# A decoder layer in one program: the end of the self-attention in a new order (layer norm and gated layer first, last output products behind the second gated tile, four weight pieces behind batch 1's rows)

## The reference

```
x = x + attention(layernorm(x))          16 heads of 64, causal, output product with w_o
x = x + cross_attention(layernorm(x))    keys and values from 64 context rows per batch
x = x + ffn(layernorm(x))

ffn: h = silu(x w1 * s1) * (x w2 * s2)   "gated layer", 256 -> 1024, 8 tiles of 128
     h = gelu(h h1 * s)                  1024 -> 1024
     h = gelu(h h2 * s)                  1024 -> 1024
     out = h w3 * s3                     1024 -> 256
```

## Time and profile before

| | us |
|---|---|
| median of 3 runs | 1507.41 |
| lowest, highest | 1506.86, 1508.65 |
| the profiled execution, its own time | 1507.81 |
| its span | 1506.0 |
| TensorE busy in the span | 1487.9 (99%) |
| VectorE, ScalarE, GpSimd busy | 1101.3, 968.6, 492.1 |

### The profile page before, as it was taken

One profiled execution on the slowest core, in us unless ns is written; L12 is line 12 of the kernel. 1 busy time (PEld: TensorE's weight loads), 2 busy tenths in 40 slices (PEclk: granted clock), 3 DMA queues, 4 the chain that ended last, 5 costly groups with the idle time before them and its releaser, 6 DMA issues.

```text
span 1506.0 us, 29162 instructions
## 1 busy us (share of the span) xinstructions
PE 1487.9 (99%) x10680; PEld 1262.7 (84%) x10680; DVE 1101.3 (73%) x2772; ACT 968.6 (64%) x2274; POOL 492.1 (33%) x763
## 2 busy tenths in 40 slices
PE   8999999999999999999998999999999999999999
PEld 6888888888888888888887788888888888888887
DVE  7999999999999899999999657555553634444443
ACT  6888888888888888888887754456444532222222
POOL 2545454445544555454453011000110212221110
PEclk9999999999999999999999999999999999999999
DMA  4000000000000000000013423421212632222221
GB/s 155 2 1 2 30 2 30 1 2 30 2 29 1 2 30 1 16 15 2 22 64 113 145 84 113 150 103 66 79 66 78 215 114 85 84 85 84 85 84 43
DMA packets 56024, 87.15 MB, mean 58 GB/s; under 512 B 4416, under 2 KB 33472, under 8 KB 55872
## 3 DMA queue, kind: packets, MB, share of 16 engines
q1 hardware_dynamic: 55872, 85.10, 16.5%
HBM read 55.72 MB, written 29.36 MB: 56 GB/s over the span
## 4 chain that ended last, share of the span: by engine, by line
PE 91%; DVE 5%; ACT 2%; DMA 1%; issue 1%; POOL 0%; SPq 0%; DVEq 0%
PE bank L1024 15%; PE bank L1026 13%; PE bank L658 10%; PE bank L578 9%; PE bank L630 8%; PE bank L580 7%; PE bank L579 7%; PE bank L642 6%; PE bank L1179 2%; PE bank L1170 2%; PE bank L1032 2%; PE bank L1146 2%; PE bank L1138 2%; PE bank L1139 2%; PE bank L1140 2%
## 5 line engine op out<-in xcount | busy, mean ns | idle before, releaser
L844 POOL TENSOR_SCALAR P<-P,stats 128x512 f32<-128x512 f32 (+3 forms) x512 | 269.0, 544 | 376.4 <-DVE stats L822 376.1
L717 ACT ACTIVATE P<-P,stats 128x384 f32<-128x384 f32 (+3 forms) x512 | 283.9, 560 | 16.4 <-DVE stats L814 16.2
L681 ACT ACTIVATE PT<-bank 128x512 fp32r<-128x512 f32 (+1 forms) x384 | 185.4, 525 | 87.6 <-PE bank L642 86.5
L814 DVE CUSTOM_DVE_ANT_0 P<-bank,cmask 128x384 f32<-128x384 f32 (+3 forms) x512 | 228.4, 483 | 1.2 <-PE bank L630 0.9
L731 DVE TENSOR_TENSOR PT<-bank,PT 128x512 fp32r<-128x512 f32 (+1 forms) x384 | 218.8, 594 | 5.3 <-ACT PT L681 4.1
L1336 DVE TENSOR_TENSOR Hb<-gt,Hb 128x512 fp32r<-128x512 f32 x128 | 90.8, 710 | 167.0 <-ACT Hb L1187 165.9
L1024 PE MATMUL bank<-Hb,hw 128*128 128x512 f32 x512 | 202.3, 395 | 0.8 <-DVE Hb L1336 0.8
L1024 PE MATMUL bank<-w,hw 128*128 128x512 f32 x512 | 199.2, 389 | 0.0
L658 PEld LDWEIGHTS bank<-PT,V 128*128 128x128 f32 x1024 | 165.0, 190 | 22.1 <-DVE PT L731 4.3
L658 PE MATMUL bank<-PT,V 128*128 128x512 f32 (+3 forms) x1024 | 176.7, 320 | 3.5 <-DVE PT L731 3.5
L1026 PE MATMUL bank<-Hb,hw 128*128 128x512 f32 x448 | 174.8, 390 | 0.0
(11 more groups left out here) (230 smaller groups left out, 3305.4 us busy)
## 6 DMA issues: line engine op xcount, KB each, us to landing
h_scratch<-go SPq DMA_DIRECT2D x64, 256.0 KB, 2.0
xs<-x_scratch SPq DMA_DIRECT2D x23, 512.0 KB, 4.1
hx<-h_scratch SPq DMA_DIRECT2D x32, 256.0 KB, 6.1
stageA<-in_h SPq DMA_DIRECT2D x14, 512.0 KB, 3.6
x_scratch<-x SPq DMA_DIRECT2D x8, 512.0 KB, 3.0
x_scratch<-xs SPq DMA_DIRECT2D x8, 512.0 KB, 2.9
qf<-h_scratch SPq DMA_DIRECT2D x16, 256.0 KB, 5.3
pf<-h_scratch SPq DMA_DIRECT2D x16, 256.0 KB, 6.0
```

What stands on the lines that cost most here:

```text
L681: return e.activation(dst, src, ACT.Copy, scale=scale)
L717: e.activation(p, p, ACT.Exp, bias=st_[:, k:k + 1], scale=-1.0, accum_out=st_[:, 8 + k:9 + k]).then_inc(s_exp, 1)
L814: e.tensor_tensor_reduce(P_tile(P, i, a), banks["S", P, max(i, 1)][a][:, slice(*S_COLS[i])], cmask[:, 512 - n:512], -1.0, 3.0e38, ALU.add, ...
L844: e.tensor_scalar(p, p, stats[P % 4][:, k:k + 1], 1.0, ALU.mult, ALU.mult).then_inc(s_norm, 1)
```

## The change

Only rows of the step lists move; no step is added, removed or altered.

- TensorE: O.63 and O.64 stand behind u.0.1 instead of ahead of g.0.0.
- VectorE: pl.63.2.0 comes ahead of os.62 and both xoa; fl.7 comes behind lsum.0.1, fl.8 behind lnorm.0.1, and both ys.63 behind that; xtl.0.1 comes ahead of xva.2 and flag.2; fl.9 to fl.11 move in among the gated tiles; os.63 and os.64 come behind hl.0.1; flag.3 comes behind hm.0.7; fl.13 to fl.16 leave this list.
- ACT: yo.63.0 and yo.63.1 come ahead of big.7; xth.0.1 comes ahead of fh.9, xvh.2 and big.8; silu.0.0 to silu.0.2 move ahead of big.10; fh.13 to fh.16 come at the end of the list, and big.13 and big.14 leave it.
- In `later()`: fl.13, fl.14 and big.13 come behind xt.1.0's steps and ahead of gelu.0.0, big.14 behind it; fl.15, fl.16 ahead of gelu.0.1, big.15 and big.16 behind it. In before, big.15 stood behind gelu.0.0 and big.16 behind gelu.0.1.

```diff
@@ TAIL "PE"
-        T.63.1 O.62 xo.0.0 xo.0.1 AV.63.0 AV.63.1 xv.2 xv.3 xt.0.1.0 xt.0.1.1 ft.2 O.63 O.64 g.0.0 u.0.0 g.0.1
+        T.63.1 O.62 xo.0.0 xo.0.1 AV.63.0 AV.63.1 xv.2 xv.3 xt.0.1.0 xt.0.1.1 ft.2 g.0.0 u.0.0 g.0.1 u.0.1 O.63
...
@@ TAIL "ACT"
-        fh.12 silu.0.5 fh.13 fh.14 big.12 hh.0.5 silu.0.6 silu.0.7 fh.15 hh.0.6 hh.0.7 fh.16 big.13 big.14""",
+        fh.12 silu.0.5 hh.0.5 silu.0.6 big.12 silu.0.7 hh.0.6 hh.0.7 fh.13 fh.14 fh.15 fh.16""",
@@ later()
-                o += [("h", 0, 0)] + also(0, ("h", 0)) + [("gelu", 0, 0), ("hst", 0, 0), ("big", 15)]
+                o += [("h", 0, 0)] + also(0, ("h", 0)) + [("fl", 13), ("fl", 14), ("big", 13), ("gelu", 0, 0), ("hst", 0, 0), ("big", 14)]
             elif (b, m) == (0, 1):
-                o += [("h", 0, 1)] + also(0, ("h", 1)) + [("gelu", 0, 1), ("hst", 0, 1), ("big", 16)]
+                o += [("h", 0, 1)] + also(0, ("h", 1)) + [("fl", 15), ("fl", 16), ("gelu", 0, 1), ("hst", 0, 1), ("big", 15), ("big", 16)]
```

More of the change, by code:

```diff
@@ L123 @@
         S.63.3 S.63.2 xv.0 xv.1 xf.0 xf.1 T.62.1 S.63.1 T.62.0 xc xs.0 AV.62.0 O.61 AV.62.1 T.63.0 T.63.2 xpt.0
-        T.63.1 O.62 xo.0.0 xo.0.1 AV.63.0 AV.63.1 xv.2 xv.3 xt.0.1.0 xt.0.1.1 ft.2 O.63 O.64 g.0.0 u.0.0 g.0.1
-        u.0.1 g.0.2 u.0.2 g.0.3 u.0.3 g.0.4 u.0.4 g.0.5 u.0.5 g.0.6 u.0.6 g.0.7 u.0.7 ft.3""",
+        T.63.1 O.62 xo.0.0 xo.0.1 AV.63.0 AV.63.1 xv.2 xv.3 xt.0.1.0 xt.0.1.1 ft.2 g.0.0 u.0.0 g.0.1 u.0.1 O.63
+        O.64 g.0.2 u.0.2 g.0.3 u.0.3 g.0.4 u.0.4 g.0.5 u.0.5 g.0.6 u.0.6 g.0.7 u.0.7 ft.3""",
     "ACT": """
@@ L144 @@
         e.63.1.1 big.5 e.63.0.0 xvh.0 xcc e.63.0.1 xvh.1 big.6 yo.62.0 xe.0 yo.62.1 ph.63.0.0 ph.63.2.1 xph.0
-        ph.63.0.1 ph.63.1.0 ph.63.1.1 ph.63.2.0 fh.7 fh.8 big.7 yo.63.0 fh.9 yo.63.1 big.8 xvh.2 fh.10 xvh.3
-        xth.0.1.0 xth.0.1.1 big.9 fh.11 big.10 silu.0.0 silu.0.1 big.11 silu.0.2 hh.0.1 silu.0.3 hh.0.3 silu.0.4
-        fh.12 silu.0.5 fh.13 fh.14 big.12 hh.0.5 silu.0.6 silu.0.7 fh.15 hh.0.6 hh.0.7 fh.16 big.13 big.14""",
+        ph.63.0.1 ph.63.1.0 ph.63.1.1 ph.63.2.0 fh.7 fh.8 yo.63.0 yo.63.1 big.7 xth.0.1.0 xth.0.1.1 fh.9 xvh.2
+        big.8 fh.10 silu.0.0 xvh.3 silu.0.1 big.9 silu.0.2 fh.11 big.10 hh.0.1 silu.0.3 hh.0.3 big.11 silu.0.4
+        fh.12 silu.0.5 hh.0.5 silu.0.6 big.12 silu.0.7 hh.0.6 hh.0.7 fh.13 fh.14 fh.15 fh.16""",
     "DVE": """
@@ L168 @@
         pl.62.0.0 pl.62.1.1 m.63.0.0 pl.62.0.1 m.63.0.1 fl.6 xvl.0 r.63.0 xs1.0 xs2.0 xs3.0 xs4.0 os.61 ys.62.0
[L169 to L172, removed]
+        xvl.1 xr.0 ys.62.1 pl.63.0.0 pl.63.2.1 xpl.0 pl.63.0.1 pl.63.1.0 pl.63.1.1 pl.63.2.0 os.62 xoa.0.0
+        xoa.0.1 lsum.0.1 fl.7 lnorm.0.1 fl.8 ys.63.0 ys.63.1 xtl.0.1.0 xtl.0.1.1 xva.2 flag.2 xva.3 fm.2 fl.9
+        xvl.2 xvl.3 hm.0.0 fl.10 hm.0.1 hl.0.0 hm.0.2 hl.0.1 os.63 os.64 hm.0.3 hl.0.2 fl.11 hl.0.3 hm.0.4
+        hl.0.4 hm.0.5 fl.12 lsum.1.0 hl.0.5 hm.0.6 hm.0.7 flag.3 lnorm.1.0 fm.3 hl.0.6 hl.0.7""",
     "POOL": """
```

## The result

| | us |
|---|---|
| the changed kernel, median of 4 runs | 1519.72 (1519.55 to 1522.85) |
| the kernel before, 4 runs beside them | 1507.57 |
| ratio, 95% interval | 1.0080 (1.0067 to 1.0092) |
| the profiled execution of the changed kernel, its span | 1519.55, 1517.7 |

The change makes the kernel slower by 12.1 us; 1521 was predicted, with 1513 to 1525 around it.

What follows compares the result with a forecast made beforehand. TensorE was taken as the bound, with holes in the 36 us from 806 to 842 and nothing behind able to absorb delay. +9.2 - 0.8 + 1.8 + 1.5 + 1.5 = +13.2 on 1507.81 gave 1521 us, range 1513 to 1525.

Steps and rivals of the forecast that it cites:

- c1: Clock fall in the hole ahead of ft.2: 1.5 us, 0 if it stays up, 1.9 at most.
- c2: Clock fall in the hole ahead of ft.3: 1.5 us, range 0 to 1.9.
- Part 1: Front of VectorE's queue: AV.63 starts 2.5 us sooner at full clock, xt.0.1 starts 4.5 us sooner.
- Part 2: Check flags: ft.2 waits for flag.2 and big.8, starts at 819.35 against 819.03; the 4.5 us are lost, clock falls.
- Part 3: O.63 and O.64 behind four gated halves: nothing won; g.0.2 at 826.6 plus c1, against 826.19.
- Part 4: Queues behind g.0.2 delay os.64, st.7, ld.12 and batch 1's rows: ft.3 9.2 us later, ends 7.5 to 10.5.
- Part 5: Pieces 13 to 16 behind batch 1's rows: four checks on ACT delay TensorE 1.8 us, between 0 and 2.5.
- 0.8 us given back: The 0.78 us hole in h.0.0 goes, as lnorm.1.0, hl.0.6 and hl.0.7 run during the wait ahead of ft.3.
- B: Rival: same waits, but the clock stays up in one or both holes, 1518 to 1519.5 us; chance 0.19.
- C: Rival: hh.0.1 does not hold VectorE, os.64 ends 4.9 us sooner and the whole chain with it, 1516 us; chance 0.09.
- D: Rival, faster: big.8 over by 816.8, flag.2 does not hold TensorE, no second hole, 1505 us; chance 0.04.
- E: Rival, worse: loads 1.5 us late and Part 5 at 2.5, or a third clock fall, 1523.5 to 1527; chance 0.12.

Runs made afterwards that it cites:

- b1: Kernel before plus the change's front, its holes covered (O.63 and O.64 ahead of ft.2; checks, norm, sums, store earlier): 1508.79 us, ratio 1.0004.
- e6: Changed kernel with big.8 ahead of fh.9 and xvh.2 on ACT, flag.2 ahead of xva.2 on VectorE: 1519.24 us, ratio 1.0075.
- e7: Changed kernel with os.63, os.64 ahead of hm.0.2 on VectorE and st.7, ld.12, xload.1 ahead of ld.14 on SyncE: 1517.75 us, ratio 1.0067.
- e1: Changed kernel with os.63 and os.64 two rows up on VectorE, ahead of hm.0.2 and hl.0.1: 1520.94 us, ratio 1.0077.
- e2: Changed kernel with the four checks and weight halves 13 to 16 back where they stood before: 1519.31 us, ratio 1.0074.
- e3: Changed kernel with unread products on TensorE in two holes, 19 ahead of ft.2 and 38 ahead of ft.3: 1517.59 us, ratio 1.0054.
- e5: Kernel before with one move, pl.63.2.0 ahead of xoa.0.0, os.62 and fl.7 on VectorE: 1508.65 us, ratio 1.0004.
- b2: b1 with lsum.1.0 and flag.3 earlier on VectorE, batch 1's rows loaded earlier, ft.3 one product pair later: 1508.18 us, ratio 1.0003.
- e4: Changed kernel with idle transposes on TensorE in two holes, 40 ahead of ft.2 and 76 ahead of ft.3: 1516.66 us in one run.

## Why the prediction was right, step by step

All in microseconds behind the marker. "Predicted" is the difference that the prediction's own steps give, with c1 and c2 where they had come in.

| step | before | after | measured | predicted |
|---|---|---|---|---|
| AV.63 starts | 7.54 | 5.03 | -2.5 | -2.5 |
| xt.0.1 | 17.22 | 12.69 | -4.5 | -4.5 |
| ft.2 | 18.15 | 18.56 | +0.4 | +0.3 |
| g.0.2 | 25.31 | 27.13 | +1.8 | +1.9 |
| st.7 | 24.36 | 33.40 | +9.0 | +9.2 |
| ld.12 | 27.38 | 36.34 | +9.0 | +9.1 |
| ft.3 | 37.16 | 47.26 | +10.1 | +10.7 |
| xt.1.0 | 42.78 | 53.80 | +11.0 | +11.4 |
| ft.0 | 56.65 | 69.64 | +13.0 | +13.2 |
| end of the span | 705.12 | 718.17 | +13.05 | +13.2 |

- **Part 1** held: AV.63 ends 4.1 us sooner, start and length together, and the norm ends 4.5 us sooner. (The prediction put sm at 810.1 where its own terms add up to 809.9; it was there at 810.1 on that clock.) lpow, which was open between 1.01 and 2.58 us and taken at 2.0, took 1.94 with fl.7 beside it; lnorm took 1.38. In b1, where VectorE ran ys.63 (one input in PSUM) beside it, the same instruction took 1.03. The timelines of GpSimd, after and b1:

```profile
808.81 1.94 POOL L1550 TENSOR_TENSOR sm<-sm,half 128x4 f32<-128x4 f32 x1 [6.00 <-DVE sm L1378]
```

```profile
810.70 1.03 POOL L1557 TENSOR_TENSOR sm<-sm,half 128x4 f32<-128x4 f32 x1 [5.99 <-DVE sm L1385]
```

 fl.7 ran from 808.64 to 809.86 and lpow ended at 810.75, 0.9 us behind it. This agrees with the rule that the prediction named from the Trainium skill ("SBUF — State Buffer", section "Who interferes with whom"), that GpSimd waits out a VectorE instruction with two SBUF inputs; with nothing to wait out it took 1.03 in b1. b1 paid for this order at once: its lnorm took 2.83 us, as in the earlier trace rows, with yh and yl on GpSimd beside it.
- **Part 2** held: the 4.5 us are gone by ft.2, and flag.2 waited 1.52 us for big.8. e6 shows that big.8's place is the cause of 1.9 us of the hole; the rest is VectorE's queue behind the norm, which the prediction's sum has too (fl.8, ys.63, xtl).
- **Part 3** held: nothing won by the place of O.63 and O.64.
- **Part 4** held as a chain, nearly row for row: g.0.2 was put at 826.6 plus c1 and the sums' end 6.2 us behind it; measured 6.25. It was 0.6 us too long at ft.3, because the piece landed after 3.1 us where 3.5 was taken, and batch 1's rows were just there when lsum.1.0 asked. What the prediction told too simply is what the chain is worth. It followed one chain through the store and the load and didn't ask what would stand right behind it; e7 took the transfers off the path and 8.2 of the 10.1 us at ft.3 stayed (7.3 without this run's longer first fall of the clock), with ACT's and VectorE's queues behind g.0.2 on the chain in their place. Its lower end of 7.5 for this term adds two landings that run side by side; by its own chain a microsecond off each makes 8.2. e1 failed on the same point: of a step that is moved, the queue that issues its transfer counts too (ld.14 ahead of st.7).
- **Part 5**: 1.97 us measured from xt.1.0 to ft.0, 1.8 predicted; e2 undoes it and gives back 2.3.
- **c1 and c2**: c1 was 1.41 (8.57 us from ft.2 to g.0.2, where before had 7.16), or 1.16 over e3, near the 1.5 taken. c2 was **mis-sized**: the stretch from ft.3 to xt.1.0 took 6.54 us, and e3 puts it at 3.84 without falls and waits, so c2 was 2.70, not 1.5 and beyond the 1.9 given as its upper end. It had been read from AV.63 alone, where the fall was over within the 5.65 us of AV.63 and xv; behind ft.3 the slow products go on for 5.8 us, to 852.6. The four other traces with a fall at both places (e1, e2, e6, e7) have it the other way round: c2 1.3 to 1.6, and c1 1.8 to 2.1 over e3. Nothing in the runs tells why c1 came out near its 1.5 in this trace and c2 did not, so the first is luck; the two together were 3.2 to 3.9 us in all five, where 3.0 was taken. The **0.8 us given back** was also too small: before took 5.62 us for this stretch, 1.78 more than e3. The two errors, +1.2 and -1.0, cancelled; together with the 0.6 at ft.3 the sum came out 0.15 us off. That the sum is so close is partly luck. It also counts c1 in full at ft.3, where e3 got only 0.7 us of it back.

Of the rivals, B (the clock stays up) fell at once, and e3 shows what it would have been worth. C (hh.0.1 doesn't hold VectorE) fell: hl.0.1 waited 1.56 us for it. Its price was wrong too: e7 has the sums and the store off that wait, st.7 went 5.4 us sooner behind g.0.2 than in after, and ft.3 followed by 2.75, not one for one. D needed big.8 over 15.9 us behind the marker (its 816.8), and it ended at 18.2. E and F didn't come about.

## What to carry to other kernels

Count what a moved step delays as closely as what it frees: here 4.5 us were won at the layer norm and all lost at the next flag, 1.9 of them because a check had got behind other steps on ACT, the rest because the steps that the norm had overtaken on VectorE now stood between it and the flag. When a hole on TensorE is removed, look where the next one opens and whether it is long enough for the clock to fall; e5, b1 and b2 each won time at one place and paid it back at the next, with VectorE's work in the stretch unchanged. And before giving a wait on a transfer the blame, ask what the chain is without it: e7 took two transfers off the path and most of the delay stayed.

## What the runs showed of the hardware that was not expected

- One fall of the clock cost between 1.2 and 2.7 us in this kernel, and not the same in the same place: from ft.3 to xt.1.0 2.70 us over e3 in after, but 1.62 in e1, 1.41 in e2, 1.49 in e6 and 1.33 in e7; from ft.2 to g.0.2 1.16 us over e3 in after, but 2.11, 1.84, 1.87 and 2.05 in these. In the rows by microsecond the clock is already at 0.50 while TensorE still idles, so how much work is caught depends on where in the hole it fell. After and e1 have the same first hole, 4.78 us: in after the clock fell some 15.6 us behind the marker and was back at 22.4, in e1 it fell at 17.6 and was back at 24.4, 2 us further into the products. A price for a fall should be a range.
- Idle transposes, 40 and 76 in a row, kept the granted clock at 1.00 through holes of 4.8 and 8.7 us (e4), as unread products did (e3).
- Two transfers of 512 KB issued 0.37 us apart: in e1 the load took 4.0 us to land and the store behind it 4.9. In after, with 2.4 us between the two, they took 3.2 and 2.9. A step that goes sooner can so make its successor later.
